# Latent attention in a decoder kernel: where the causal bias is added to the scores, and how the router's last batches are ordered

## The reference, cut to what matters

```python
def _L1_attn_ref(hidden_states, Wq, Wkvc, Wkdec, Wvdec, Wqrope, Wkrope, Wo):
    c = hidden_states @ Wkvc                       # 64 latent features per token
    ...                                            # q, k from x and c, 16 heads
    scores = jnp.einsum('bqhd,bkhd->bhqk', q, k) * scale
    causal = jnp.tril(jnp.ones((s, s), dtype=bool))
    scores = jnp.where(causal[None, None], scores, jnp.finfo(scores.dtype).min)
    attn = jax.nn.softmax(scores, axis=-1)
    out = jnp.einsum('bhqk,bkhd->bqhd', attn, v_p).reshape(b, s, H * FULL)
    return out @ Wo

def _L1_ffn_ref(x, w_gate, w1, w3, w2):            # softmax router, best 2 of 8 experts
    logits = SOFTCAP * jnp.tanh(x @ w_gate / SOFTCAP)
    ...
```

## Time and profile before

| what | value |
|---|---|
| median of 3 runs | 740.68 us (739.47 to 741.49) |
| the profiled execution | 740.18 us, its span in the trace 738.3 us |
| instructions | 13918 |
| busy of the span: PE, PEld | 89%, 73% |
| busy of the span: DVE, ACT, POOL | 66%, 59%, 27% |
| latent attention, first to last score maximum | 384.1 to 517.9 us |
| from there to the experts' first tile | about 67 us |

### The profile page before, as it was taken

How to read it: one execution, slowest core, us unless ns; L and a number is a source line. 1 busy time by engine, 2 the same in 40 slices (tenths; PEclk the granted TensorE clock), 3 DMA queues, 4 the chain that set the end, 5 groups by cost and what they waited for, 6 DMA issues and landing times.

```text
span 738.3 us, 13918 instructions
## 1 busy us (share of the span) xinstructions
PE 653.8 (89%) x4832; PEld 538.7 (73%) x4833; DVE 487.7 (66%) x1091; ACT 436.0 (59%) x1124; POOL 200.2 (27%) x364
## 2 busy tenths in 40 slices
PE   7788787998998998987999999999978899999950
PEld 5566677998998898873467887888865478787840
DVE  2577776469478477539887857576555587777725
ACT  4998847338448457446878756475342366666612
POOL 3455520031000000000224434444137313232314
PEclk9999899999999999999999999999999999999995
DMA  8997000220220223130011000000095211111114
GB/s 305 383 327 198 1 1 1 90 90 1 90 90 1 90 90 115 60 113 1 1 39 49 2 1 2 2 1 1 13 426 232 66 36 50 50 49 51 44 59 140
DMA packets 32226, 62.03 MB, mean 84 GB/s; under 512 B 2500, under 2 KB 26824, under 8 KB 29928
## 3 DMA queue, kind: packets, MB, share of 16 engines
q1 hardware_dynamic: 30152, 56.04, 22.4%
q0 software_dynamic: 2016, 5.22, 2.0%
HBM read 45.80 MB, written 15.55 MB: 83 GB/s over the span
## 4 chain that ended last, share of the span: by engine, by line
PE 65%; ACT 13%; DVE 13%; issue 3%; DMA 3%; POOL 3%; SPq 0%; POOLq 0%; ACTq 0%; DVEq 0%
PE banks L1758 41%; PE bank L1758 24%; ACT arena L766 4%; DVE U_split L1234 3%; ACT U_split L785 2%; DVE mx L1188 1%; POOL xs L670 1%; DMA ys<-arena 1%; ACT arena L804 1%; DVE fh L1411 1%; DVE arena L1408 1%; POOL rstd L574 1%; DMA arena<-ys 1%; DVE bmx L1253 1%; ACT arena L978 1%
## 5 line engine op out<-in xcount | busy, mean ns | idle before, releaser
L1758 PE MATMUL banks<-U_split 128*128 128x512 f32 (+1 forms) x616 | 146.8, 350 | 5.2 <-DVE U_split L1234 3.1
L1758 PE MATMUL bank<-U_split 128*128 128x256 f32 (+1 forms) x864 | 116.2, 291 | 13.8 <-DVE U_split L1234 13.7
L1758 PEld LDWEIGHTS bank<-U_split 128*128 128x128 f32 x864 | 109.1, 195 | 17.7 <-issue 15.5
L1758 PEld LDWEIGHTS banks<-U_split 128*128 128x128 f32 x616 | 96.4, 189 | 23.1 <-issue 8.0
L785 ACT ACTIVATE U_split<-arena 128x1024 fp32r (+6 forms) x122 | 97.3, 821 | 13.6 <-DVE arena L1676 4.9
L1758 PE MATMUL banks<-cst,arena 128*128 128x128 f32 (+1 forms) x594 | 90.6, 280 | 6.2 <-DVE arena L1196 3.1
L571 POOL TENSOR_SCALAR rstd<-mv 128x1 f32<-128x1 f32 x48 | 11.0, 229 | 294.5 <-DVE mv L1166 262.2
L1758 PE MATMUL banks<-arena 128*128 (+4 forms) x632 | 85.3, 386 | 4.8 <-DVE arena L1182 3.9
L1758 PEld LDWEIGHTS banks<-cst,arena 128*128 128x128 f32 (+1 forms) x594 | 69.7, 143 | 18.6 <-POOL arena L602 3.7
L1758 PEld LDWEIGHTS banks<-arena 64*128 64x128 f32 (+3 forms) x632 | 61.4, 178 | 22.5 <-issue 7.6
L1024 ACT ACTIVATE arena<-banks,dmx 128x128 f32<-128x128 f32 (+1 forms) x128 | 52.9, 424 | 38.6 <-DVE dmx L1515 38.6
(11 more groups left out here) (236 smaller groups left out, 1187.3 us busy)
## 6 DMA issues: line engine op xcount, KB each, us to landing
arena<-in_w_exp SPq DMA_DIRECT2D x8, 1536.0 KB, 14.1
xs<-arena SPq DMA_DIRECT2D x8, 1032.0 KB, 14.0
arena<-in_ctxT SPq DMA_DIRECT2D x4, 1601.0 KB, 6.7
arena<-in_ctx SPq DMA_DIRECT2D x4, 1536.0 KB
arena<-in_w_f SPq DMA_DIRECT2D x3, 1024.0 KB, 11.5
arena<-xs SPq DMA_DIRECT2D x23, 129.0 KB, 2.0
w_x<-in_w_x SPq DMA_DIRECT2D x9, 256.0 KB, 7.4
arena<-in_w_oh SPq DMA_DIRECT2D x1, 2048.0 KB, 8.6
```

The costliest lines, as they stand in the source:

```text
L1758: return nc.tensor.matmul(o, w, x, start=start, stop=stop, **k)
```

## The change

The bias leaves TensorE. `d_mask` is gone; its waits for a free bank move to the head of `d_scores`, whose matmuls now start their own sums instead of adding to the bias. DVE adds the bias in the score bank, in place, over the two diagonal blocks of each head (128 x 256), after the wait for the scores and ahead of the two maxima; `link` makes DVE wait for the add's end before the maxima. `cbias` and the values are the same.

In the router part three things move. `e_rstd` now waits for both rows of a batch and does the add and the power on two columns at once, then the two negated means one by one; for this the constant `mhalf` has two columns. `r_scatter(1)` is cut: three of its four scatters before the layernorm of batch 3, the fourth behind it. On TensorE `e_out(3)` goes ahead of the wait and the transpose `to_xT(3, 2)`.

```diff
@@ -189,7 +189,7 @@
         cbias = sb("cbias", [P, 3 * P], BF16)
         ones = sb("ones", [P, P])
         magic = sb("magic", [P, 1])
-        mhalf = sb("mhalf", [P, 1])
+        mhalf = sb("mhalf", [P, TPB])
 
         x_ids = sb("x_ids", [P, NT, E + 2])
         x_row = x_ids[:, :, 0:E]
@@ -571,7 +571,7 @@
                 g.tensor_scalar(rstd[:, s:s + 1], mv[:, s, 1:2], LN_EPS, None, ALU.add).then_inc(G["pool_step"], 1)
                 steps[0] += 1
                 pool.wait_ge(G["pool_step"], steps[0])
-                g.tensor_tensor(rstd[:, s:s + 1], rstd[:, s:s + 1], mhalf[:, :], ALU.pow).then_inc(G["pool_step" if centre else "ln_rstd"], 1)
+                g.tensor_tensor(rstd[:, s:s + 1], rstd[:, s:s + 1], mhalf[:, 0:1], ALU.pow).then_inc(G["pool_step" if centre else "ln_rstd"], 1)
                 if centre:
 
                     steps[0] += 1
@@ -655,30 +655,41 @@
                     for t in range(TPB):
                         rstd_of(3 * NT + 2 * (b - 1) + t)
             def e_rstd(n):
-                for t in range(TPB):
-                    rstd_of(n + t, centre=True)
-
-            def r_scatter(b):
+
+                both = slice(n % 4, n % 4 + TPB)
+                pool.wait_ge(G["ln_var"], n + TPB)
+                g.tensor_scalar(rstd[:, both], mv[:, both, 1], LN_EPS, None, ALU.add).then_inc(G["pool_step"], 1)
+                steps[0] += 1
+                pool.wait_ge(G["pool_step"], steps[0])
+                g.tensor_tensor(rstd[:, both], rstd[:, both], mhalf[:, :], ALU.pow).then_inc(G["pool_step"], 1)
+                steps[0] += 1
+                pool.wait_ge(G["pool_step"], steps[0])
+                for s in (n % 4, n % 4 + 1):
+                    g.tensor_scalar(nmr[:, s:s + 1], mv[:, s, 0:1], rstd[:, s:s + 1], -1.0, ALU.mult, ALU.mult).then_inc(G["ln_rstd"], 1)
+
+            def r_scatter(b, parts):
                 pool.wait_ge(G["r_rows"], 2 * b + 2)
                 pool.wait_ge(G["ln_done"], 4 * NT + 2 * b + 2)
                 if b == 0:
                     pool.wait_ge(G["const_set"], 10)
-                for t in range(2 * b, 2 * b + 2):
-                    for c in range(TOPK):
-
-                        z = E + 1 + c
-                        g.indirect_dma_start(xs_words, bass.IndirectOffsetOnAxis(ap=tok_rows[:, c, t:t + 1], axis=0),
-                                             x_ids[:, t, 0:z], None).then_inc(G["r_scat"], 16)
+                for n in parts:
+                    t, c = 2 * b + n // TOPK, n % TOPK
+
+                    z = E + 1 + c
+                    g.indirect_dma_start(xs_words, bass.IndirectOffsetOnAxis(ap=tok_rows[:, c, t:t + 1], axis=0),
+                                         x_ids[:, t, 0:z], None).then_inc(G["r_scat"], 16)
 
             e_rstd(4 * NT - 2)
             e_rstd(4 * NT)
             e_rstd(4 * NT + 2)
-            r_scatter(0)
+            every = range(TPB * TOPK)
+            r_scatter(0, every)
             e_rstd(4 * NT + 4)
-            r_scatter(1)
+            r_scatter(1, every[:3])
             e_rstd(4 * NT + 6)
-            r_scatter(2)
-            r_scatter(3)
+            r_scatter(1, every[3:])
+            r_scatter(2, every)
+            r_scatter(3, every)
 
 
             def m_ids(i):
@@ -884,7 +895,7 @@
                     if c == 1 and b + 1 < B:
                         b_split_q(b + 1)
                 if b + 1 == B:
-                    a.activation(fs[:, 0, 7:8], mhalf[:, :], ACT.Sigmoid)
+                    a.activation(fs[:, 0, 7:8], mhalf[:, 0:1], ACT.Sigmoid)
                 if b + 1 < B:
                     b_split_k(b + 1)
                     c_split(b + 1)
@@ -1511,6 +1522,8 @@
                     for h in (2 * p, 2 * p + 1):
                         dve.wait_ge(G["d_s"], h + 1)
                         bank = score_bank(h)
+                        diagonal = bank[:, 0:4 * P].rearrange("p (j c k) -> p j c k", j=2, c=2)[:, :, 0, :]
+                        link(v.tensor_tensor(diagonal, diagonal, cbias[:, 0:P].unsqueeze(1).broadcast_to([P, TPB, P]), ALU.add))
                         v.tensor_reduce(dmx[:, h % 8, 0:1], bank[:, 0:P], AX, ALU.max, negate=True).then_inc(G["d_max"], 1)
                         v.tensor_reduce(dmx[:, h % 8, 1:2], bank[:, P:3 * P], AX, ALU.max, negate=True).then_inc(G["d_max"], 1)
                 if p == 0:
@@ -2240,27 +2253,21 @@
                     to_xT(1, 0)
             f_hiddenT(NT - 1)
 
-            def d_mask(p):
-
+            def d_scores(p):
+
+                b = p // PAIRS
                 for h in (2 * p, 2 * p + 1):
                     if h < 3:
                         pe.wait_ge(*((G["d_c_sb"], 2), (G["f_h"], 2 * NT), (G["f_sig"], 2 * NT))[h])
                     else:
                         pe.wait_ge(G["d_exp"], 2 * (h - 3) + 2)
-                    diagonal = score_bank(h)[:, 0:4 * P].rearrange("p (j c k) -> p j c k", j=2, c=2)[:, :, 0, :]
-                    mm(diagonal, ident16[:, :], cbias[:, 0:P].unsqueeze(1).broadcast_to([P, TPB, P]), stop=False)
-
-            def d_scores(p):
-
-                b = p // PAIRS
                 pe.wait_ge(G["d_q_sb"], p + 1)
                 pe.wait_ge(G["d_c_sb"], 2 * b + 1)
                 for t in reversed(range(TPB)):
                     for i in range(2):
                         at = slice(i * LAT, (i + 1) * LAT)
                         ins = mm(score_bank(2 * p + i)[:, t * P:(2 * t + 1) * P], qe[at, p % 3, t * P:(t + 1) * P],
-                                 cT[at, b % 2, 0:(t + 1) * P], start=False, stop=t == 0, tile_position=(i * LAT, 0),
-                                 skip_group_check=t == 1)
+                                 cT[at, b % 2, 0:(t + 1) * P], tile_position=(i * LAT, 0))
                         if t == 0:
                             ins.then_inc(G["d_s"], 1)
 
@@ -2410,7 +2417,6 @@
                     pe.wait_ge(*((G["d_c_sb"], 2 * b + 4) if b + 1 < B else (G["ln_var"], 3 * NT + 2 * b)))
                     to_xT(2, b - 1)
                 if p < NP:
-                    d_mask(p)
                     d_scores(p)
                 if 3 <= p < NP + 3:
                     d_values(p - 3)
@@ -2451,9 +2457,9 @@
             e_gate(3)
             r_count(1)
             e_transpose(3)
+            e_out(3)
             pe.wait_ge(G["xT_done"], 3 * B + 2)
             to_xT(3, 2)
-            e_out(3)
             r_logits(2)
             keep_clock(9)
             r_count(2)
```

## The result

| | us | ratio to before |
|---|---|---|
| before, median of 11 runs | 741.45 (739.47 to 744.21) | |
| changed kernel, median of 11 runs | 746.01 (742.97 to 749.58) | 1.0067 [1.0044, 1.0091] |
| profiled execution of the changed kernel | 745.71, its span 743.8 | |

The change is slower by 0.67%. The forecast was 741.2, no change that can be measured; the median is 4.8 us above it, on the side that had a chance of 0.33. It lies inside the range (to 746.5) by 0.5 us, and five of the eleven executions lie above it.

The account below looks back on a forecast made before the run. TensorE was taken as the bound, with DVE's loop taking over in plain pairs. From 740.18, attention +1.5 (4.1 + 0.3 - 2.5 - 1.9 - 0.9 + 2.4) and router -0.95 gave 740.7, as a median 741.2 us; range 736.5 to 746.5.

Parts of the forecast that it names:

- the loop: Plain pair: maxima, ACT's exps, DVE's reciprocal and weight copy take 3.22 us; the even head's add makes it 3.68.
- A: DVE's price for one add in PSUM up to its waiting successor: 0.46 us, bounds 0.34 and 0.92.
- Rival 3: DVE's add in PSUM costs more than 0.53 us; at 0.70 the kernel takes 749.0; chance 0.17.
- Rival 1: DVE's wait on its own add is free (A = 0.34): -2.9 us, 738.3 in all; chance 0.12.
- Rival 2: TensorE stays the attention's bound, so all 32 pairs' masks are gained: -9.9 us, 730.1 in all; chance 0.07.
- The mask matmuls that go: Two mask matmuls per pair on TensorE, 0.31 us of each pair, at most 9.9 us over 32 pairs.
- The turn pairs: Two intervals of 3.82 us with a layernorm end on DVE behind the maxima come to 3.99: +0.3.
- The lead: TensorE enters each run of projection pairs 0.63 us early, cashed in three times: -1.9.
- rival 4: The lead does not exist: TensorE's transposes wait for POOL's scalings, or values for DVE's split; 743.7 us; chance 0.16.
- The first interval: Batch 0, pair 0 to 1: ends 0.1 us earlier, mask gone and the activation table load hiding the adds.
- Rival 5: The router's part of the change gives 0 in place of -0.95 us: 742.2 in all; chance 0.08.
- step (c): Router: later logits and clock-keeping matmuls limit the gain; the last transpose moves from 568.98 to 568.0, -0.95 us.

Follow-up runs that it names:

- no_bias: Kernel before's router; in the changed attention the bias is left out on both engines, so neither masks nor adds; one execution 735.31 us.
- even_add: Kernel before's router; DVE adds the bias for even heads only, TensorE keeps the mask for odd heads; one execution 747.52 us.
- odd_add: Kernel before's router; DVE adds the bias for odd heads only, TensorE keeps the mask for even heads; one execution 740.59 us.
- late_turn: Attention's part of the change, router as before, with TensorE's transposes of the layer's input moved behind the scores at q = 7; one execution 744.63 us.
- filled: Attention's part of the change, router as before, plus eight unneeded matmuls in TensorE's gap ahead of pair 1's scores; 745.66 us, ratio 1.0066 to before.
- router_only: Only the router's part of the change, TensorE laying the bias as in the kernel before; 741.15 us, ratio 0.9995 to before.

## Why the prediction was right or wrong

**What bounds the kernel, and the loop: right.** The loop of 3.22 stands in `no_bias` as 3.21 to 3.22, with one even add it is 3.68, forecast and measured; 14 intervals give +4.06 for +4.1. That the odd head's add is free was read from 0.99 against 1.10; `even_add`, as long as the kernel with both adds, and `odd_add` show it.

**The price of the add: right.** A was taken as 0.46 from the add of equal width and source, and is 0.46; writing to PSUM adds nothing that shows. Rival 3 (over 0.53) is out. Rival 1 (a free link, 0.34) would have made plain pairs 3.56; they are 3.68, and the linked successor comes 0.12 to 0.13 later than an unlinked one (0.46 against 0.34 and 0.33), so it is out too. The Trainium skill (VectorE: DVE Perf Modes, section "The DRAIN you can't avoid") states that a semaphore between two operations costs nothing extra. The trace disagrees with that rule by these numbers.

**Rival 2 was out for the reason given**: only 0.17 of waiting stood in the round, and TensorE lost its place as the bound.

**The mask matmuls that go: the first term that failed.** The prediction took the time from the first mask to the first score, 0.31, as what the edit gives back. The runs give 0.21. It counts where TensorE is the bound, or where the masks stand in the ring: 0.8 in eight projection pairs, 0.3 in the four intervals of batch 0 (two adds less the masks are 0.92 - 0.21 = 0.71 and not 0.61; measured 0.61, 0.71, 0.71, 0.70), and 0.1 each in the sixth interval and the last. That is 1.3 of the 3.1 us by which the attention's sum fell short.

**The turn pairs: wrong, 0.8.** The layernorm's end on DVE (L1182) was seen behind the maxima and counted on DVE alone: "by the same count they come to 3.99". Its reader was not looked up. TensorE's transposes wait for it, with the scores of the next pair behind them in order; two adds push it back, and TensorE idles 0.59. `late_turn` takes the wait off the path and gets 3.88. The same wait sits in the last interval: 4.41, and 3.98 without it, where 3.95 was forecast. Of the 3.1 us this is 0.8 in the turns and some 0.4 in the last interval.

**The lead: right, and 0.1 too large.** The first projection pair of each run takes 0.53 less than the next (5.52 against 6.05), where 0.63 was forecast. At the first of them the chain of waits turns from DVE to TensorE through what rival 4 named, POOL's scaling ahead of TensorE's transposes:

```profile
463.08 0.84 POOL arena L647 x2
...
463.96 1.59 PE banks L1771 x12
```

TensorE idles 0.29 there. The rival priced this at the whole lead; it took at most a sixth of it. That the missing 0.1 is this wait is read from the chain and was not tested.

**The first interval: wrong, 0.3.** "The activation table load hides the adds" does not hold. ACT waits for the even head's maxima and only then loads the table:

```profile
385.72 1.28 ACT L1035 ACT_TABLE_LOAD   x1 [0.41 <-DVE dmx L1528]
```

The maximum that it waits for ends at 385.64. Pair 0's even add is not in the interval only because it stands ahead of the first maximum. Pair 1's is in it, since it stands ahead of the second, and brings 0.46 (4.67 in `even_add`, where it was 4.21). Some 0.22 comes back from the odd head's mask, which stood between ACT's exps and the scores (3.99 in `odd_add`). That makes about +0.2, with +0.19 measured, where -0.1 was forecast.

**The clock: not in the prediction at all.** Batch 0 was costed in intervals at full clock. The longer gaps that the adds leave on TensorE there went with a fall of the clock in four of six traces, worth 1.76 when it comes. By the traces alone, attention +4.6, two times in three another 1.8, and router -0.8 make about +5.0; the medians are 4.6 apart, the ratio says 5.0 with an interval from 3.3 to 6.7. `filled` did not confirm that share.

**The router: right.** -0.95 was forecast; the part differs by 1.22 between the first two traces, some 0.4 of which is the last pair's add and not the router, and like for like by 0.6 to 0.9, once by 1.1. Rival 5 (nothing) has the traces against it; the runs of `router_only` alone can't exclude it. POOL, then TensorE, in the trace of the changed kernel, against the earlier trace rows:

```profile
569.75 0.23 POOL L661 TENSOR_SCALAR rstd<-mv 128x2 f32<-128x2 f32 x1 [0.77 <-DVE mv L1603]
570.06 0.72 POOL L664 TENSOR_TENSOR rstd<-rstd,mhalf 128x2 f32<-128x2 f32 x1
570.88 0.55 POOL L668 TENSOR_SCALAR nmr<-mv,rstd 128x1 f32<-128x1 f32 x2
571.60 1.07 POOL L679 DMA_INDIRECT xs<-x_ids,arena  x1 [0.17 <-issue]
...
572.00 1.46 PE L1771 MATMUL banks<-w_ff,ident 128*128 128x512 bf16 x6
...
573.29 0.60 PE L1771 MATMUL bank<-cst,x_ids 128*128 128x128 f32 x4
```

Both rows go through one add and one power, the held-back scatter comes behind them, and POOL is done with the layernorm 1.68 after it starts (569.75 to 571.43) where it took 2.56 (565.64 to 568.20). The final transpose no longer waits for ACT: the clock-keeping matmuls stand ahead of it, as step (c) said. It comes 50.43 after the last pair's first maximum, before 51.63.

**The chances.** The sign was the weak point. The attention's +1.5 was the rest of +6.8 and -5.3. The losses lay in waits that were read from rows; the gains supposed that TensorE would cash in every gap it was given, and each of them came out smaller. The forecast's own spread was put on both sides alike, where it belonged on slower. That the time still lies in the range is in part luck. The range reached up to 746.5 for a dearer add (rival 3) and a lead that does not exist (rival 4). The add was not dearer and most of the lead was there; masks worth less, the turns and the clock used up that room instead.

## What to carry to other kernels

Moving work to an engine with spare time is priced by the loop in which it lands, not by its busy share: DVE had 28% to spare in batch 1, in a plain pair one add was free and the other, equally long, made 3.68 of 3.39. Put it behind the result that the other engines wait for (here the odd head), and leave it on the old engine where the ring already goes through the new one. For every operation that is pushed back, look up who reads it, and for every matmul removed, how much later its successor could have started anyway.

## What was not expected of the hardware

- Two bf16 matmuls of 256 columns take 0.31 from start to the next start, and taking them out gives 0.21 or 0.22: each is worth 0.10 to 0.11.
- A DVE instruction that waits for the one before it by a semaphore starts 0.46 after it, one that does not starts after 0.33 or 0.34, behind instructions of 0.41 and 0.42.
- The clock of TensorE fell to half for 6.8 us behind idle times of 1.55 and 0.53, in four of six traces, and not in the first trace of the changed kernel and that of `late_turn`, whose gaps were the same (1.55, then 0.54 and 0.53). What decides is open.
- POOL's power takes 0.72 on two columns and 0.56 or 0.57 on one in the router, so pairing two rows saves 0.4 on it.
- ACT's table load (1.28) starts only 0.08 after the end of the maximum for which the next exp waits; ACT had been idle for 0.41 before it.
- An add in place in PSUM takes DVE 0.42 to 0.43 for 256 columns, the same as one that only reads PSUM.
